# A fourth input buffer in the normalisation stage of a fused attention and routed-FFN kernel

## The reference

```python
xn = _layernorm(x, axis=-1)                      # x: (8, 4096, 1024) float32
s = _L0_attn_ref(xn, Wq, Wk, Wv)                 # 16 heads of 64, causal after the softmax
g = _silu(_L0_ffn_ref(xn, sim_matrix, gates, q_proj, k_proj, v_proj, o_proj))
x = x + s * g
```

## Time and profile before

| what | value |
|---|---|
| median of the runs | 3648.35 us (3645.08 to 3651.63, two runs) |
| the profiled execution's own time | 3645.8 us |
| its span (first to last instruction, slowest core) | 3644.1 us |
| around the span | 1.7 us |
| spans of the eight cores | 3629.0 to 3644.1 us |
| TensorE, DVE, ACT busy, share of the span | 70%, 62%, 58% |

### The profile page before, as it was taken

How to read it: one execution, slowest core, us unless ns; L and a number is a source line. 1 busy time by engine, 2 the same in 40 slices (tenths; PEclk the granted TensorE clock), 3 DMA queues, 4 the chain that set the end, 5 groups by cost and what they waited for, 6 DMA issues and landing times.

```text
span 3644.1 us, 59738 instructions; the slowest of 8 cores (3629.0 to 3644.1 us)
## 1 busy us (share of the span) xinstructions
PE 2533.6 (70%) x18500; PEld 1152.7 (32%) x18642; DVE 2273.4 (62%) x5890; ACT 2123.9 (58%) x2466; POOL 255.2 (7%) x706
## 2 busy tenths in 40 slices
PE   1107999657657777777877777777777777776551
PEld 1103444323323333333333333333333333332220
DVE  4434777314336677677667667766766766776764
ACT  0000000351107798789679778878977977897662
POOL 0010000000000000001001000100100000011112
PEclk9999999789978877876786787688687777765555
DMA  3241000011130000000000000000000000002345
GB/s 93 75 121 35 1 1 1 1 47 47 72 125 3 3 6 6 4 3 9 3 4 6 5 3 4 7 3 4 9 3 3 6 5 4 4 7 82 132 142 200
DMA packets 35776, 117.11 MB, mean 32 GB/s; under 512 B 5778, under 2 KB 5778, under 8 KB 35474
## 3 DMA queue, kind: packets, MB, share of 16 engines
q1 hardware_dynamic: 22738, 71.34, 5.8%
q0 software_dynamic: 12736, 41.95, 3.9%
HBM read 79.72 MB, written 33.55 MB: 31 GB/s over the span
## 4 chain that ended last, share of the span: by engine, by line
PE 31%; ACT 20%; issue 13%; DVE 12%; DMA 9%; another core or an unknown queue 9%; DVEq 4%; POOL 1%; ACTq 0%; SPq 0%; POOLq 0%
ACT expC L1333 7%; ACT stagef L1348 5%; PE PB L880 5%; PE PB L894 5%; PE PB L865 4%; DMA stagef<-x 4%; PE PB L797 4%; PE PB L752 3%; PE PB L794 3%; ACT stagef L1333 3%; PE PB L809 3%; DVE tmpc L1197 3%; ACT R L1348 2%; DVEq L1265 2%
## 5 line engine op out<-in xcount | busy, mean ns | idle before, releaser
L1197 DVE TENSOR_REDUCE tmpc<-stagef 128x2 f32<-128x1024 bf16 (+2 forms) x726 | 811.2, 1126 | 236.3 <-ACT stagef L1348 179.4
L1333 ACT ACTIVATE expC<-PB 128x1024 bf16<-128x1024 f32 x768 | 860.1, 1120 | 86.9 <-PE PB L880 86.9
L1348 ACT ACTIVATE stagef<-PB 128x1024 bf16<-128x1024 f32 x600 | 673.6, 1123 | 202.9 <-PE PB L894 134.9
L1197 DVE TENSOR_REDUCE tmpc<-R 128x2 f32<-128x1024 bf16 (+2 forms) x362 | 406.1, 1122 | 118.3 <-ACT R L1348 89.9
L1333 ACT ACTIVATE stagef<-PB 128x1024 bf16<-128x1024 f32 x384 | 432.8, 1127 | 71.3 <-PE PB L880 71.3
L880 PE MATMUL PB<-R 64*128 64x512 bf16 x1152 | 297.9, 505 | 229.5 <-ACT stagef L1348 134.3
L880 PE MATMUL PB<-QTt,KTt 64*128 64x512 bf16 x1152 | 284.5, 482 | 147.2 <-ACT stagef L1348 79.3
L1348 ACT ACTIVATE R<-PB 128x1024 bf16<-128x1024 f32 x296 | 332.8, 1124 | 81.5 <-PE PB L894 58.8
L680 PE MATMUL PB<-R,xnT 128*128 128x512 bf16 x1504 | 336.8, 381 | 3.0 <-DVE lnat L990 1.3
L1313 ACT ACTIVATE expC<-PB 128x512 bf16<-128x512 f32 x144 | 83.6, 596 | 397.8 <-remote 343.1
L894 PE MATMUL PB<-R 64*128 64x512 bf16 (+3 forms) x1088 | 262.8, 475 | 40.1 <-ACT expC L1333 22.4
(11 more groups left out here) (162 smaller groups left out, 2943.2 us busy)
## 6 DMA issues: line engine op xcount, KB each, us to landing
stagef<-x SPq DMA_DIRECT2D x64, 512.0 KB, 4.4
out<-Vau SPq DMA_DIRECT2D x32, 512.0 KB, 3.3
g_sp<-stagef SPq DMA_DIRECT2D x32, 256.0 KB, 2.0
s_sp<-s_stage POOLq DMA_DIRECT2D x64, 128.0 KB, 2.4
QTt<-g_sp POOLq DMA_DIRECT2D x32, 256.0 KB, 4.6
KTt<-s_sp POOLq DMA_DIRECT2D x32, 256.0 KB, 5.2
R<-qp POOLq DMA_DIRECT2D x8, 512.0 KB, 5.3
R<-kp POOLq DMA_DIRECT2D x8, 512.0 KB, 4.6
```

The source lines that it names most:

```text
L1197: e.tensor_reduce(s.tmpc[:].rearrange("p (h c) -> p h c", h=2)[:, :, c:c + 1], s.c1scr((m1 - 1) % 3)[:, 0:2 * kw] .rearrange("p (h k) -> p ...
L1333: e.activation(s.expCs(es), PB[[0, 1, 3][it["slot"]]][:, :], AF.Exp).then_inc(sem["aC2"], 1)
L1348: e.activation(scr[:, 0:1024], pbsrc[:, 0:1024], AF.Exp).then_inc(sem["aC1"], 1)
```

## The change

The x loop gets a fourth buffer, columns 3072 to 4095 of `stagef`, with a fourth semaphore, `dX21`. Load i now waits, from load 4 on, for `vXN >= i - 3`, that is for tile i - 4 to be normalised. Four loads are issued at the start without a wait. DVE reads its tiles from the four buffers in turn. The buffer `sq8` has to leave those columns and moves to `s_stage`, by which its element type goes from float32 to bf16. The final counts of the semaphores follow. No engine's instructions are added, removed or put in another order; what differs is addresses, the waits, and one output type.

```diff
-        s.sq8 = s.stage[0:8, 3072:4096]
+        s.sq8 = s.s_stage[0:8, 0:1024]
...
-            xb3 = [s.stage[:, 0:1024], s.stage[:, 1024:2048], s.stage[:, 2048:3072]]
-            dxs = ["dX0", "dX1", "dX20"]
+            xb3 = [s.stage[:, 0:1024], s.stage[:, 1024:2048],
+                   s.stage[:, 2048:3072], s.stage[:, 3072:4096]]
+            dxs = ["dX0", "dX1", "dX20", "dX21"]
             for i in range(NT):
-                if i >= 3:
-                    e.wait_ge(sem["vXN"], i - 2)
-                e.dma_start(xb3[i % 3], xr[:, i, :]).then_inc(sem[dxs[i % 3]], 16)
+                if i >= 4:
+                    e.wait_ge(sem["vXN"], i - 3)
+                e.dma_start(xb3[i % 4], xr[:, i, :]).then_inc(sem[dxs[i % 4]], 16)
...
-            finals.update(dX0=16 * 11, dX1=16 * 11, dX20=16 * 10,
+            finals.update(dX0=16 * 8, dX1=16 * 8, dX20=16 * 8, dX21=16 * 8,
...
                 e.tensor_scalar(s.xnb[:, (j % 2) * 1024:(j % 2) * 1024 + 1024],
-                                xb3[j % 3], s.Dup[:, 2 * j:2 * j + 1],
+                                xb3[j % 4], s.Dup[:, 2 * j:2 * j + 1],
...
-                e.wait_ge(sem[dxs[i % 3]], 16 * (i // 3 + 1))
-                e.bn_stats(bn6[:, 0:6], xb3[i % 3][:, 0:512])
-                e.bn_stats(bn6[:, 6:12], xb3[i % 3][:, 512:1024])
+                e.wait_ge(sem[dxs[i % 4]], 16 * (i // 4 + 1))
+                e.bn_stats(bn6[:, 0:6], xb3[i % 4][:, 0:512])
+                e.bn_stats(bn6[:, 6:12], xb3[i % 4][:, 512:1024])
```

## The result

| | before | after |
|---|---|---|
| median of the runs | 3656.91 us (3645.08 to 3707.83, 10 runs) | 3561.18 us (3551.71 to 3628.98, 11 runs) |
| ratio, 95% interval | | 0.974 [0.969, 0.979] |
| profiled execution, span of the slowest core | 3644.1 us | 3563.4 us |

The change makes the kernel 2.6% faster.

The account below looks back on a forecast made before the run. The x loop was bound by DVE waiting for x transfers, one load in flight at a time. Saving 94 us there, with the start, squares and semaphores at 0, gave 3645.8 - 94, about 3552 us; range 3538 to 3585.

Parts of the forecast that it names:

- The sum: x loop, worked out tile by tile: tile 31's statistics at 118.35 us instead of 212.4, saving 94 us.
- The recursion: x loop: each tile starts at the later of DVE's pace and issue plus flight plus 0.09 us; tile 31 at 118.35.
- The wait: DVE's wait for x transfers at line 951 should fall from 99.5 us to between 5 and 15.
- The two limits: x loop, per tile: DVE's own round 3.28 us, the transfer 3.37 us; nearly coinciding, so neither alone gives the answer.
- The start: Four x loads with two weight loads at the start: fourth landed by about 15 us, needed at 19.6, so hidden.
- The squares: Squares written as bf16 ahead of tile 0 on DVE: between 0.9 us gained and 1.2 lost, taken as 0.
- The later stages: Behind the x loop: tail 8.4, weight stretch 71 and dense stage 330 us keep their lengths, about 94 us earlier.
- rival B: Attention stage: another mixture of clock levels gives back part of the saving, 1% being 22 us (3574); chance 0.06.
- Rival A: x loop: loads in flight slow each other down, only 82 to 56 us saved, 3564 to 3590 us; chance 0.14.
- the nearest row: Weight stretch, two loads in flight: 4.6 to 4.7 us to landing against 3.6; 0.9 us more per flight saves 82.
- Rival C: PE's dense projections: a share stays at 1.2 GHz, making it slower than before, up to 3882 us; chance 0.02.
- Rival D: x loop: `vXN` or a landing order holds load i to the old moment, time stays at 3646 us; chance 0.02.

Follow-up runs that it names:

- the repeated profile: The changed kernel as it is, run once more on the chip of the other follow-up runs; the profiled execution took 3598.3 us, ratio to before 0.981.
- the run that was held back: The changed kernel with four buffers, each load from load 4 on waiting one tile later, as before the change; ratio to before 1.002.

## Why the prediction was right

*The sum.* Forecast 3552 us, range 3538 to 3585; the median is 3561.2 and the ratio 0.974 of the 3648.35 us then shown is 3553.5. The recursion gave tile 31 at 118.35 us; core 5 has it at 118.32, core 0 at 120.06, all cores between 113.9 and 120.1. Part of that agreement is luck, since the flights of another execution fell elsewhere: in the repeated profile tile 31 starts at 113.5 to 118.2 us. The wait was to be 5 to 15 us, and 6.9 in the sum. It was 5.6 on core 5 and 7.7 on core 0, but 2.4 to 4.7 on cores 2, 3 and 4, and 1.6 to 5.2 in the repeated profile. So that term was sized a few us too high for most cores: its flights were those of core 0, the core with nearly the longest wait before, with their two of over 5 us.

*The two limits.* That DVE's floor is 3.28 us a tile is shown by the run with five buffers, which starts tile 31 at 110.3 to 111.4 where 111.5 was worked out. That the moment of issue decides is shown by the run that was held back.

*The start.* The first wait came at tile 4, at 23.39 us, 0.39 us long. Four x loads landed after 8.8 us at the median and 12.6 at the longest, the two weight loads after 11.4. DVE took the fourth tile without a wait: hidden, as said.

*The squares.* 0 us, within 0.01 us of each instruction.

*The later stages.* The tail, the weight stretch and the dense stage keep their lengths. On core 5 tile 31 came 93.4 us earlier and the whole span was 78.3 us shorter; 12 of the 15 us between them were lost ahead of the attention stage, whose first matmuls (line 881, before the change 880) start at 1008.6 us instead of 1090.2. The same part of that stretch, core 5 before, then core 5 and core 6 of the changed kernel:

```profile
1053.00:1073.00 20.00, 17.17 (x88) 7.76 (x87) 7.80 (x21) 0.00 (x0) 0.00 (x0) 1.00 0.00 0
...
960.00:980.00 20.00, 17.17 (x74) 7.23 (x74) 6.51 (x19) 0.00 (x0) 0.00 (x0) 0.81 0.00 0
...
960.00:980.00 20.00, 17.06 (x86) 7.75 (x87) 7.80 (x21) 0.00 (x0) 0.00 (x0) 1.00 0.00 0
```

Core 5 had the clock 0.81 from about 850 to 900 us and from about 950 to 1009 us, and core 4 beside it too (0.81 for 960 to 1000 us), while core 6 had 1.00. In the repeated profile core 5 shows 1.00 for 949 to 999 us and lost 4 us over the whole span, not 15. The attention stage itself, from the first to the last matmul of that line, took 2511.9 us before and 2517.5 after on core 5, 2509.3 and 2508.1 on core 0. So rival B's mechanism, another mixture of the two levels in the attention stage, cost nothing or a few us; what core 5 gave back came from a clock of 0.81, a level that the prediction didn't have, ahead of that stage. No profile of a kernel with the old timing of the loads has it there, but the repeated profile of the changed kernel hasn't either, so nothing shows that the change brings it. What sets it was not tried.

*Rival A* was wrong for the change and right as a mechanism. Median landing was 3.5 to 3.9 us over the eight cores before and 3.5 to 4.0 with loads one round further ahead, at most 0.4 us more on one core, since a flight of under 4 us issued every 3.4 us hardly overlaps. On core 0 it reached 5.0 at 238 GB/s and 7.5 at 277 GB/s, and 6.9 with four weight loads in flight. The weight stretch that I had used as the nearest row (4.7 us) overstated it for this loop.

The Trainium skill's fit ("DMA: Bandwidth & Descriptors", "Anatomy of one DMA": 2.0 us plus bytes / 436e3, so 3.2 us by estimate) is given there for loads that GpSimd issues, which the prediction left out; the x loads leave from SP. It would have had tile 31 at 111.5; the trace has 113.9 to 120.1 with landing at 3.5 to 4.0, so the measured flights were the better base. The Trainium skill, "HBM Reference", "Latency", lets an access rise to 2 us at high load; the flights at 277 GB/s are 3.9 us longer than at 77, so the direction agrees and the size here is larger, though landing also holds whatever time a load spends behind the core's other loads, and no run here separates the two.

*Rival C* did not occur in the profiled execution: all eight cores show 1.00 for 230 to 550 us. Its place was well chosen all the same: the dense stage did run at a lower clock on two cores of the repeated profile and cost them 55 us, at 0.82 on the mean and not at the 0.50 of 1.2 GHz by which the rival was priced (last section). *Rival D* is excluded by the trace.

## What to carry to other kernels

Ask of a ring of buffers not how many it has but in which round a buffer is let go: with the consumer two tiles behind, three buffers are one, and the fourth was worth 95 us of 3648. Work out the loop as a recursion (the later of the engine's own pace and issue plus flight), check it on the trace before, and then read off what one more buffer gives, what two give, and where it stops. More loads in flight also lengthen each flight: in the weight stretch four buffers took out 25 of 70 us while landing went from 4.7 to 6.9. Moving those loads under another engine's work took out nearly all the rest, as long as the ring of x buffers had the lead to absorb the longer flights.

## What the runs showed of the hardware

The dense stage, PE busy throughout, can run at a lower clock on just two neighbouring cores. In the run with the squares alone, 353 to 640 us, cores 0, 1 and 2:

```profile
353.00:640.00 287.00, 287.00 (x1161) 122.18 (x1160) 199.22 (x601) 0.00 (x0) 0.00 (x0) 0.84 0.00 1
...
353.00:640.00 287.00, 287.00 (x1160) 122.05 (x1158) 199.37 (x601) 0.00 (x0) 0.00 (x0) 0.84 0.00 1
...
353.00:640.00 287.00, 285.53 (x1332) 128.58 (x1358) 227.51 (x704) 0.00 (x0) 0.00 (x0) 1.00 0.00 1
```

Cores 0 and 1 get 0.84 on the mean where core 2 gets 1.00. That is no mixture of the levels of 1.2 and 2.4 GHz, 0.50 and 1.00. Core 0 in stretches of 5 us, and core 2 in the first of them:

```profile
400.00:405.00 5.00, 5.00 (x20) 2.07 (x19) 3.38 (x10) 0.00 (x0) 0.00 (x0) 0.81 0.00 0
500.00:505.00 5.00, 5.00 (x20) 2.07 (x19) 3.43 (x10) 0.00 (x0) 0.00 (x0) 0.81 0.02 3
660.00:665.00 5.00, 5.00 (x22) 2.10 (x21) 3.39 (x11) 0.00 (x0) 0.00 (x0) 0.81 0.01 2
...
400.00:405.00 5.00, 4.95 (x26) 2.32 (x25) 3.91 (x12) 0.00 (x0) 0.00 (x0) 1.00 0.00 0
```

The projection's matmuls take 437 ns at the median on core 0 and 379 on core 2, while the shortest and the longest are alike (376 and 631 ns, 376 and 634). So 0.81 is a level of its own, held for most of the stage, and 0.84 is that level with some stretches at 1.00. From its first projection matmul to its last this stage takes 397 us on core 0 (304.1 to 700.7) and 340 on core 2 (305.9 to 645.4), so it costs 57 us, more than half of what the change gains. The same shows on cores 6 and 7 of the changed kernel's second profile (0.82 for 230 to 550 us), on cores 6 and 7 of the kernel with four weight buffers (364 and 366 us for the stage against 340), and, ahead of the attention stage, on cores 4 and 5 of the changed kernel's first profile. PE had the same work before the stage on all of them. It occurs in kernels with the old and the new timing of the loads, so nothing here makes it an effect of the change. What makes it fall on one pair and not on the others stays open.
